# A patch-selection kernel that stores every tile first and finishes the kept rows afterwards by indirect transfers

## The chip, the cores and the metric

One core of a Trainium2 chip runs the whole program. The metric is device time in microseconds (us); lower is better. Before the change the median of three runs is 2007.05 us (2005.89 to 2010.34).

The core has TensorE (PE), VectorE (DVE), ScalarE (ACT), GpSimd (POOL) and SyncE (SP), which only issues transfers here. They run their own instruction lists and meet at semaphores. Indirect transfers, which gather or scatter rows by a list of row numbers, are issued by POOL.

## The reference

The input x is four images of 256 channels by 256 x 256 pixels, float32. A patch is 32 x 32 pixels, so an image has 8 x 8 = 64 places, each with one patch per channel. With `g = groupnorm(x)`:

```python
s = 0.5 * (|g[.., w+1] - g[.., w-1]| + |g[h+1, ..] - g[h-1, ..]|) + 0.5 * |g|   # zero padding of g
sp = mean of s over each 32 x 32 patch            # one score per channel and place
mask = (rank of sp among the 256 channels of the place) < 128
out = x + g * mask                                # mask is spread over the patch
```

The norm has 32 groups of 8 channels; mean and variance are over the group. A kept patch becomes `x * (1 + scale) + shift`, with scale and shift of its group, and the 128 patches that are not kept in a place are a plain copy of x.

## The kernel before

x lies in device memory as 64 tiles (16 per image) of 128 partitions by 8192 numbers, 4 MiB each. A tile is 16 channels by 8 bands of rows (the partitions) and 8 patches of 1024 pixels side by side (the free dimension). One row of 1024 numbers (4 KiB) is a patch in one partition; the indirect transfers move such rows.

**Analysis of a tile.** DVE takes the statistics (16 `bn_stats` of 512 columns, helper `statistics`, L911) one tile ahead; PE averages the mean over the group (`mean`, L680), and DVE writes its negative (`minus_mean`, L918). Then for each of the 8 patches: the sum of |x - mean| is made by ACT (L872, eight to a tile); the vertical differences by PE for 5 patches into PSUM (L707, L709), by DVE for one (L925) and by POOL for two (L355); the horizontal differences by POOL for all 8 (L349) into the buffers `pair` and `scratch`. The absolute values of the differences are summed by ACT (L866, L846, L855, L860) or by DVE (`place_sum`, L938). Columns and rows at the patches' edges have helpers of their own (L377 and L943, L689 to L696 and L948).

**Ranking.** After 16 tiles POOL and PE make the scale of each group; DVE multiplies the sums by it (`score`, L1080 and L1082), PE moves the scores so that the 64 places lie in partitions and the 256 channels in columns (L774), and DVE takes the 128 largest of each row in 16 rounds of `max` and `match_replace` (L1104, L1106). PE turns the mask back (L783), and DVE writes the coefficients (L1121 to L1126).

**Finishing, images 0 to 2.** While the next image is analysed, the tiles of the last one are read once more, in halves of 2 MiB, into three buffers `again`; ACT applies scale and shift to the whole half, kept or not (L803), and SP stores it. This is done for 27 halves of an image and, from the buffer `kept`, for its last tile. The 12 patches between are stored unchanged by a copy within device memory, and only their kept rows are gathered (L396), finished (L822) and scattered (L406). The constants `COPIES` place the 29 copies of halves in image 0, which has nothing else to finish.

**Finishing, image 3.** Ten tiles are copied within device memory early, and their kept rows are gathered, finished and scattered at the end (L521, L832, L530); the other six are finished as halves by DVE (L1178).

**Order.** It is written out by hand. ACT's list for a tile is a string such as `ORDER` (L102): `a` is a |x - mean| patch, `v` a vertical difference from PSUM, `o` a half to finish (4 instructions), `p` a group of gathered patches. POOL's list is `differences` (L411): it fills a first buffer and `scratch`, with at most one or two scatters behind the second of these, and the gathers behind the edge columns. Loops over tiles run through a ring of three buffers and `kept`.

Of the kernel before, what the change touches and what calls it, by code (L numbers as in the profile page):

```python
# [30 lines left out]

RING = 3
SLOTS = 3
LOOPED = (TILES - 1) // RING
LAST = TILES - 1
BN = 512
CHUNKS = PIX // BN

# [4 lines left out]
HALVES = 27  # L43
SPARSE_BETWEEN = [(h // 2, h % 2 * HALF_COLS + w) for h in range(HALVES, 2 * LAST) for w in range(HALF_COLS)]
SPARSE_STEP, SPARSE_GROUPS = 2, (1, 1, 1, 1, 1, 1, 1, 1, 2, 2)
assert sum(SPARSE_GROUPS) == len(SPARSE_BETWEEN) and sum(SPARSE_GROUPS[::2]) == sum(SPARSE_GROUPS[1::2])
PER_IMAGE = HALVES + 2
TURNS = HALVES // SLOTS

INSIDE = (PATCH - 2) * PATCH
PE_PATCHES = 5
DOWN_DVE, DOWN_POOL = 5, (6, 7)

PAIR_A, PAIR_B, SINGLE = range(3)
CONTENTS = {(PAIR_A, 0): (0, 1), (PAIR_A, 1): 7, (PAIR_B, 0): 6, (PAIR_B, 1): (3, 4), (SINGLE, 0): 2, (SINGLE, 1): 5}  # L60

ROUNDS = KEPT // 8
REC = 3 + COLS
INNER_ACROSS, INNER_DOWN, CENTRED, ROWS_AT_EDGE, COLUMNS_AT_EDGE = range(5)
KINDS = 5

ROWS = IMAGES * TILES * PARTS * COLS
NOT_A_ROW = 2 * ROWS
SPARSE_FIRST, SPARSE_END = 4, LAST - 1
SPARSE = SPARSE_END - SPARSE_FIRST
SPARSE_ORDER = [SPARSE_END - 2, SPARSE_END - 1, *range(SPARSE_FIRST, SPARSE_END - 2)]
SPARSE_BUFFERS = (0, 1, 2, 0, 3, 1, 2, 0, 3, 1)
SPARSE_PROGRAM = "S0 S1 G2 G3 G4 S2 G5 S3 G6 S4 G7 S5 G8 S6 G9 S7 S8 S9".split()
DENSE = [(LAST - 1, 0), (LAST - 1, 1), (LAST, 0), (LAST, 1), *((t, h) for t in range(SPARSE_FIRST) for h in range(2))]  # L80
DENSE_THERE = 4

MOVES_BEFORE_STORE = {4: 2, 5: 3, 6: 5, 7: 8, 8: 10, 9: 12, 10: 15, 11: 16}
MOVES_BEFORE_LOAD = {7: 4, 8: 6, 9: 9, 10: 11, 11: 13}
assert SPARSE_ORDER[:2] == [LAST - RING, LAST - RING + 1] and len(SPARSE_ORDER) == len(SPARSE_BUFFERS) == SPARSE


COPIED = [*(2 * TILES * (IMAGES - 1) + h for h in range(2 * SPARSE_FIRST, 2 * SPARSE_END)),
          *(2 * TILES * image + h for image in range(IMAGES - 1) for h in range(HALVES, 2 * LAST))]
COPIES = (0, 0, 1, 2, 2, 1, 2, 2, 1, 2, 2, 1, 1, 2, 2, 8)  # L90
assert sum(COPIES) == len(COPIED)


OUT, OUT_RANKING = (0, 2, 2, 2, 1, 2, 2, 1, 2, 2, 1, 2, 2, 2, 2, 0), 2
assert sum(OUT) + OUT_RANKING == HALVES and HALVES % SLOTS == 0

ORDER_FIRST = "A0 S0 d a0 B0 v0 a1 a2 v1 v2 a3 a4 a5 a6 v3 a7 v4".split()
ORDER = "o v0 a0 a1 a2 a3 a4 v1 a5 v2 d o a6 a7 v3 p v4".split()  # L102
ORDER_FIRST_LAST = "a0 v0 A0 a1 S0 v1 d a2 B0 a3 v2 a4 a5 v3 a6 a7 v4".split()
ORDER_LAST = "a0 v0 a1 v1 d a2 a3 v2 a4 a5 v3 a6 a7 v4".split()
ORDER_AFTER_RANKING = "a0 A0 v0 a1 d B0 v1 a2 A1 a3 v2 a4 a5 B1 a6 v3 a7 k k S0 S1 v4".split()


def halves_of(step):

    counts = (*OUT, OUT_RANKING)  # L110
    return range(sum(counts[:step]), sum(counts[:step + 1]))


def group_of(step):

    n = step - SPARSE_STEP
    return n if 0 <= n < len(SPARSE_GROUPS) else None


def patches_of(n):  # L120

    first = sum(SPARSE_GROUPS[:n])
    return [(p, *SPARSE_BETWEEN[p], n % 2 * HALF_COLS + p - first)
            for p in range(first, first + SPARSE_GROUPS[n])]


def patches_until(n, every=1):

# [3 lines left out]
def groupnorm_patch_topk(nc: bass.Bass, x: bass.AP, out: bass.AP):  # L132

    ctx = ExitStack()
    with ctx:
# [764 lines left out]
        def _(dve):  # L900
            def settle():
                dve.drain()  # L902
# [307 lines left out]
```

## Time and profile before

| | |
|---|---|
| median of 3 runs | 2007.05 us |
| span of the profiled execution | 2002.3 us |
| own time of it outside the span | about 4.8 us, the median less the span |
| PE, DVE, ACT, POOL busy | 1380.7, 1542.1, 1629.1, 1555.6 us |
| moved by DMA | 780.77 MB, mean 390 GB/s |
| row numbers of images 1 and 3 written (L1133, L1129) | at 867.9 and 1793.4 us |

The span runs from the first to the last instruction. A row of the page that ends in "x480 | 548.2, 1142" has 480 instructions, 548.2 us busy, 1142 ns each. In a timeline the first two columns are start and duration in us; durations of neighbours overlap by some 0.1 us, so what one instruction costs is the distance from its start to the next start. No engine is busy to the full, and the DMA engines are nearly so from 100 us to 1750 us.

### The profile page before, as it was taken

What the parts mean: (1) busy time and instruction counts of PE and PEld (TensorE: products, weight loads), DVE (VectorE), ACT (ScalarE), POOL (GpSimd) and SP (SyncE); (2) the same over time, 40 slices, a digit from 0 to 9 for tenths busy, and PEclk for the clock granted to TensorE, in tenths of its full rate; (3) what the DMA queues carried; (4) which work ended last, traced back from release to release, by engine and by line L of the source; (5) the groups of instructions that cost most, each with busy time, mean ns of one, the idle gap of its engine ahead of it and who ended that gap; (6) DMA issues with size and microseconds to landing.
All of it is one profiled execution on the core that took longest, in us unless ns stands there. A gap on an engine that the chain in (4) does not pass through costs nothing.

```text
span 2002.3 us, 16132 instructions
## 1 busy us (share of the span) xinstructions
PE 1380.7 (69%) x3528; PEld 675.7 (34%) x3528; DVE 1542.1 (77%) x2087; ACT 1629.1 (81%) x2437; POOL 1555.6 (78%) x1113
## 2 busy tenths in 40 slices
PE   5989989868768867857787687768688876820000
PEld 2444444434333433423333333334333333410000
DVE  7878898789898869879898977888888977872110
ACT  4999999898879888888898879889789887851643
POOL 7899899768787777758877868758878786746776
PEclk9999999988889878879888788889788887965555
DMA  5899899999999999998999999999999999969997
GB/s 252 330 399 369 333 360 392 354 403 424 429 432 430 422 362 433 390 415 365 428 430 429 432 399 389 433 389 386 430 430 432 426 400 390 381 267 397 397 368 270
DMA packets 72082, 780.77 MB, mean 390 GB/s; under 512 B 21883, under 2 KB 21883, under 8 KB 35648
## 3 DMA queue, kind: packets, MB, share of 16 engines
q1 hardware_dynamic: 40896, 723.54, 87.3%
q0 software_dynamic: 31104, 56.45, 7.5%
q14 instruction: 68, 0.56, 0.1%
q8 instruction: 14, 0.23, 0.0%
HBM read 568.33 MB, written 329.25 MB: 448 GB/s over the span
## 4 chain that ended last, share of the span: by engine, by line
issue 20%; DMA 19%; DVE 17%; POOL 16%; ACT 15%; PE 9%; DVEq 3%; POOLq 1%; ACTq 0%; SPq 0%
DVE stats L911 8%; DMA again<-in_x_dram 8%; POOL pair L349 5%; DMA ring<-in_x_dram 4%; ACT again L803 4%; DMA out_dram<-again 4%; DVE sums L938 4%; PE vertical L707 4%; ACT thrown L872 4%; PE vertical L709 4%; POOL pair L355 3%; DVEq L902 3%; ACT vertical L866 3%; DMA ring<-in_x_dram,pair 2%; POOL scratch L349 2%
## 5 line engine op out<-in xcount | busy, mean ns | idle before, releaser
L707 PE MATMUL vertical<-ring,plus 128*128 128x512 f32 (+1 forms) x1200 | 664.4, 638 | 241.9 <-ACT vertical L866 240.9
L349 POOL TENSOR_TENSOR pair<-ring 128x960 f32<-128x960 f32 x360 | 638.3, 1793 | 26.0 <-DVE scratch L1082 17.9
L709 PE MATMUL vertical<-ring,minus 128*128 128x512 f32 (+1 forms) x1200 | 634.0, 612 | 0.0
L911 DVE BATCH_NORM_STATS2 stats<-ring 128x6 f32<-128x512 f32 x960 | 582.4, 680 | 40.4 <-DMA ring<-in_x_dram 31.9
L872 ACT ACTIVATE thrown<-ring,record 128x1024 bf16<-128x1024 f32 x480 | 548.2, 1142 | 8.8
L938 DVE TENSOR_REDUCE sums<-pair 128x2 f32<-128x1920 f32 (+1 forms) x212 | 455.0, 2146 | 126.8 <-POOL pair L349 126.2
L803 ACT ACTIVATE again<-again,coef 128x1024 f32<-128x1024 f32 x324 | 374.4, 1227 | 107.2 <-DMA again<-in_x_dram 106.9
L707 PEld LDWEIGHTS vertical<-ring,plus 128*128 128x128 f32 x1200 | 240.9, 211 | 514.6 <-ACT vertical L866 292.4
L355 POOL TENSOR_TENSOR pair<-ring 128x960 f32<-128x960 f32 x120 | 270.5, 2254 | 141.8 <-DVE sums L938 116.3
L709 PEld LDWEIGHTS vertical<-ring,minus 128*128 128x128 f32 x1200 | 250.0, 208 | 295.5 <-issue 295.5
L349 POOL TENSOR_TENSOR scratch<-ring 128x960 f32<-128x960 f32 x120 | 215.3, 1794 | 152.8 <-ACT kept L822 103.3
L866 ACT ACTIVATE vertical<-vertical 128x960 f32<-128x960 f32 x320 | 303.6, 949 | 30.6 <-PE vertical L709 30.5
L832 ACT ACTIVATE ring<-ring,coef 128x1024 f32<-128x1024 f32 x64 | 73.1, 1226 | 114.5 <-DMA ring<-in_x_dram,pair 55.6
L925 DVE TENSOR_TENSOR vertical<-ring 128x960 f32<-128x960 f32 x60 | 109.0, 1817 | 39.4 <-ACT vertical L866 39.4
L938 DVE TENSOR_REDUCE sums<-scratch 128x1 f32<-128x960 f32 x106 | 119.1, 1123 | 4.2 <-POOL scratch L349 4.2
L1178 DVE TENSOR_SCALAR again<-again,coef 128x1024 f32<-128x1024 f32 x32 | 24.0, 822 | 121.2 <-DMA again<-in_x_dram 97.2
L680 PE MATMUL rank_bank<-record,averager 128*128 128x1 f32 x128 | 24.0, 257 | 119.6 <-DVE record L914 119.5
L530 POOL DMA_INDIRECT out_dram<-ring,pair x64 | 65.1, 1017 | 49.0 <-ACT ring L832 32.0
L872 ACT ACTIVATION_READ_ACCUMULATOR thrown<-ring,record 128x1 f32 x480 | 89.6, 187 | 0.0
L377 POOL TENSOR_TENSOR edges<-ring 128x448 f32<-128x448 f32 x60 | 81.5, 1359 | 0.8
L822 ACT ACTIVATE kept<-kept,coef 128x1024 f32<-128x1024 f32 x36 | 43.7, 1228 | 40.1 <-DMA kept<-in_x_dram,between_rows 40.1
L680 PEld LDWEIGHTS rank_bank<-record,averager 128*128 128x128 f32 x128 | 23.0, 207 | 152.3 <-DVE record L914 127.5
(118 smaller groups left out, 1443.2 us busy)
## 6 DMA issues: line engine op xcount, KB each, us to landing
ring<-in_x_dram SPq DMA_DIRECT2D x59, 4096.0 KB, 20.4
again<-in_x_dram SPq DMA_DIRECT2D x89, 2048.0 KB, 16.6
out_dram<-again SPq DMA_DIRECT2D x89, 2048.0 KB, 16.3
out_dram<-in_x_dram SPq DMA_DIRECT2D x29, 2048.0 KB, 28.6
kept<-in_x_dram SPq DMA_DIRECT2D x4, 4096.0 KB, 22.7
out_dram<-kept SPq DMA_DIRECT2D x8, 2048.0 KB, 13.8
ring<-in_x_dram SPq DMA_DIRECT2D x4, 1024.0 KB, 7.8
out_dram<-ring SPq DMA_DIRECT2D x2, 2048.0 KB, 9.7
```

The lines of the kernel that those rows point to most:

```text
L349: return nc.gpsimd.tensor_tensor(part.rearrange("p (r c) -> p r c", r=PATCH), xs[:, w, :, 2:], xs[:, w, :, 0:PATCH - 2], ALU.subtract)
L355: return nc.gpsimd.tensor_tensor(part, v[:, 2 * PATCH:], v[:, 0:INSIDE], ALU.subtract)
L377: nc.gpsimd.tensor_tensor(between.rearrange("p (w k r) -> p w r k", k=2, r=PATCH), xs[:, 1:, :, 0:2], xs[:, 0:COLS - 1, :, PATCH - 2:], AL ...
L707: nc.tensor.matmul(v[:, first:end], plus[:], xs[:, first + 2 * PATCH:end + 2 * PATCH], start=True, stop=False)
L709: done = nc.tensor.matmul(v[:, first:end], minus[:], xs[:, first:end], start=False, stop=True)
L803: done = nc.scalar.activation(v, v, ACT.Identity, scale=coef[:, bass.ds(t, 1), 0, w:w + 1].rearrange("p a w -> p (a w)"), bias=coef[:, bas ...
L832: nc.scalar.activation(v, v, ACT.Identity, scale=coef[:, t, 0, w:w + 1], bias=coef[:, t, 1, w:w + 1]).then_inc(sparse_finished, 1)
L866: done = nc.scalar.activation(v, v, ACT.Abs, accum_out=sums[r][:, INNER_DOWN, k:k + 1])
L872: nc.scalar.activation(thrown[:], patch(buffer, k), ACT.Abs, bias=record[r][:, 2:3], accum_out=sums[r][:, CENTRED, k:k + 1]).then_inc(cent ...
L911: nc.vector.bn_stats(stats[:, k, :], buffer[:, k * BN:(k + 1) * BN])
L925: nc.vector.tensor_tensor(down_dve, v[:, 2 * PATCH:], v[:, 0:INSIDE], ALU.subtract)\
L938: nc.vector.tensor_reduce(out, place[b], over, ALU.add, apply_absolute_value=True)\
```

## The change

The new kernel computes the same and is laid out anew. What changes, part by part:

1. **Storing.** Every tile is stored unchanged from the ring (`store_tile`) as soon as it is there, in all four images. Nothing is loaded a second time as halves, and nothing is copied within device memory (`COPIES` is all zero). The ring has four buffers. Excepted are "dense" tiles (`DENSE_FROM`): the last tile of images 0 to 2 and the last four of image 3 stay in the ring until their coefficients exist, are finished there and stored.
2. **Finishing.** For each of the 64 places of an image one indirect transfer gathers the 128 kept rows of the other tiles (partition = rank in the place), one ACT instruction finishes them, and one indirect transfer scatters them over the stored copy. Four places are a block; a block takes one of three buffers `slots`. A tile's step of image 1, 2 or 3 carries one block: POOL scatters block n-2 and gathers block n, ACT finishes block n-1. The 16 blocks of image 3 follow at the end.
3. **Lists.** DVE also writes which channels were picked (`max_index` in each of the 16 rounds, turned by PE in `turn_order`), the row numbers, and scale and shift of each picked row (`factors_of`, four times an image).
4. **Horizontal differences.** |a - b| is summed as 2 max(a, b) - a - b: DVE makes the sum of the maxima with one `scalar_tensor_tensor` with `accum_out` per patch (8 to a tile), and the sums of a and b come from the statistics and from the end columns (POOL adds 512 of them, DVE sums). POOL keeps three vertical differences a tile and ACT sums them. `place_sum` and its reductions on DVE, and DVE's own vertical difference, are gone. Only for the first tile of images 1 to 3, analysed beside the ranking, does POOL make all eight horizontal ones, with ACT summing.
5. **Loops** over tiles are unrolled.

```diff
-RING = 3
-SLOTS = 3
+RING = 4
+DENSE_FROM = (LAST, LAST, LAST, TILES - RING)
+COPIES = (0,) * TILES
+BLOCK = 4
+SETS = 3
-ORDER = "o v0 a0 a1 a2 a3 a4 v1 a5 v2 d o a6 a7 v3 p v4".split()
+ORDER = "p0 a0 v0 a1 p1 a2 o0 v1 a3 a4 o1 p2 v2 a5 o2 a6 v3 o3 a7 v4".split()
...
+            def gather_block(n):
+                image, first = n // BLOCKS, n % BLOCKS * BLOCK
+                pool.wait_ge(rows_ready, image + 1)
+                if n >= SETS:
+                    pool.wait_ge(scattered[n % SETS], 16 * BLOCK * blocks_before(n))
+                for j in range(BLOCK):
+                    row = rows[image % 2][:, first + j:first + j + 1]
+                    nc.gpsimd.indirect_dma_start(slot(n, j), None, x_rows,
+                                                 bass.IndirectOffsetOnAxis(ap=row, axis=0), bounds_check=ROWS - 1,
+                                                 oob_is_err=False).then_inc(gathered[n % SETS], 16)
...
+            for tile in range(ALL_TILES):
+                image, t = tile // TILES, tile % TILES
+                n = tile - TILES
+                if n >= 2:
+                    scatter_block(n - 2)
+                wait_loaded(pool, tile)
...
+                else:
+                    if n >= 0:
+                        gather_block(n)
+                    difference(tile, 0)
+                    end_columns(tile)
+                    difference(tile, 1)
+                    columns_at_edge(tile)
+                    difference(tile, 2)
...
+            scatter_block(STREAMED - 2)
+            scatter_block(STREAMED - 1)
+            for n in range(STREAMED, ALL_BLOCKS):
+                gather_block(n)
+                if n >= STREAMED + 1:
+                    scatter_block(n - 1)
+            scatter_block(ALL_BLOCKS - 1)
...
+            def store_tile(tile):
+                wait_loaded(sp, tile)
+                sp.dma_start(out[tile], ring[tile % RING][:]).then_inc(stored[tile % RING], 16)
...
+                for w in patches:
+                        nc.vector.scalar_tensor_tensor(out=larger[w % 2][:].rearrange("p (r c) -> p r c", r=PATCH),
+                                                       in0=xs[:, w, :, 2:], scalar=0.0, in1=xs[:, w, :, 0:PATCH - 2],
+                                                       op0=ALU.add, op1=ALU.max, accum_out=maxima[:, w:w + 1])
...
-                for _ in range(ROUNDS):
+                for k in range(ROUNDS):
                     nc.vector.max(largest[:], left)
                     settle()
+                    nc.vector.max_index(picked[:, 8 * k:8 * k + 8], largest[:], left)
                     nc.vector.match_replace(out=left, in_to_replace=largest[:], in_values=left, imm_value=-1.0)
```

DVE's step of a tile after the change, in its order: statistics of the next tile in four parts, the eight horizontal patches in four pairs between them, `keep_sums` of the tile before (which waits until ACT has done that tile), the end columns, edge rows, the negative mean of the next tile, edge columns, three small sums.

POOL before, in a step of images 1 to 3 (L349 and L355 fill buffers for the tile, L406 scatters, L396 gathers):

```order
L349 TENSOR_TENSOR pair<-ring 128x960 [waits place_free0]
L349 TENSOR_TENSOR pair<-ring 128x960
L402 ISA [waits copied]
L349 TENSOR_TENSOR scratch<-ring 128x960 [waits place_free2,between_finished]
L406 DMA out_dram<-kept,between_rows 65536x1024
L376 REGISTER_ALU
L377 TENSOR_TENSOR edges<-ring 128x7x32x2 [waits edges_free]
```

There two of the tile's differences stand ahead of the wait on `between_finished`, and one transfer follows it. POOL now, one step of images 1 to 3 and the start of the next (L372 scatters, L357 gathers, L320 makes a vertical difference, L333 the end columns, L343 to L347 the edge columns):

```order
L372 DMA out_dram<-slots,rows 65536x1024 [waits finished]
L372 DMA out_dram<-slots,rows 65536x1024 x3
L357 DMA slots<-in_x_dram,rows 128x1024 [waits scattered0,rows_ready,loaded2]
L357 DMA slots<-in_x_dram,rows 128x1024 x3
L320 TENSOR_TENSOR place<-ring 128x960 [waits place_free]
L333 TENSOR_TENSOR ends<-ring 128x512 [waits edges_free]
L320 TENSOR_TENSOR place<-ring 128x960 [waits place_free]
L343 TENSOR_TENSOR edges<-ring 128x7x32x2 [waits edges_free]
```

Eight transfers stand ahead of the tile's first difference, and the first of them waits for `finished`. ACT now, the end of one tile's list and the start of the next (L623 finishes a place, L653 sums one of POOL's differences, L659 one of PE's, L666 is |x - mean|):

```order
L666 ACTIVATE thrown,sums<-ring,record 128x1024 [waits centred]
L659 ACTIVATE vertical,sums<-vertical 128x960 [waits vertical_ready]
L623 ACTIVATE slots<-slots,offset,factor 128x1024
L666 ACTIVATE thrown,sums<-ring,record 128x1024 [waits centred]
L659 ACTIVATE vertical,sums<-vertical 128x960 [waits vertical_ready]
L653 ACTIVATE place,sums<-place 128x960 [waits place_ready,recorded]
L666 ACTIVATE thrown,sums<-ring,record 128x1024 [waits centred,minus_mean_ready]
```

The last place of a block (L623, which raises `finished`) stands two instructions ahead of the tile's end, and the next tile's list opens with a difference of POOL (L653), where before it opened with a half to finish.

## Rows read from the trace of the kernel before

**Rows 1.** The page, part 1 (engines' busy us) and part 2: GB/s in 40 slices.

```profile
PE 1380.7 (69%) x3528; PEld 675.7 (34%) x3528; DVE 1542.1 (77%) x2087; ACT 1629.1 (81%) x2437; POOL 1555.6 (78%) x1113
...
GB/s 252 330 399 369 333 360 392 354 403 424 429 432 430 422 362 433 390 415 365 428 430 429 432 399 389 433 389 386 430 430 432 426 400 390 381 267 397 397 368 270
```

**Rows 2.** The page, part 4: the chain that ended last, by engine.

```profile
issue 20%; DMA 19%; DVE 17%; POOL 16%; ACT 15%; PE 9%; DVEq 3%; POOLq 1%; ACTq 0%; SPq 0%
```

**Rows 3.** Stretches: us, busy PE, PEld, DVE, ACT, POOL, clock, DMA share, GB/s.

```profile
500.00:600.00 100.00, 71.17 (x172) 33.94 (x171) 86.83 (x108) 84.00 (x123) 81.47 (x56) 0.87 1.01 431
...
1850.00:1900.00 50.00, 0.00 (x0) 0.00 (x0) 8.88 (x12) 30.03 (x27) 35.79 (x37) 0.50 1.02 397
```

**Rows 4.** Groups of POOL by form: xcount | busy us, mean ns | idle before.

```profile
L355 POOL TENSOR_TENSOR pair<-ring 128x960 f32<-128x960 f32 x120 | 270.5, 2254 | 141.8 <-DVE sums L938 116.3 <-ACT pair L860 24.7
...
L396 POOL DMA_INDIRECT kept<-in_x_dram,between_rows x36 | 40.2, 1118 | 6.6 <-issue 6.6
L406 POOL DMA_INDIRECT out_dram<-kept,between_rows x36 | 39.8, 1104 | 6.5 <-issue 5.9
```

**Rows 5.** Timeline of POOL at the end: start, duration, instruction, idle before.

```profile
1884.33 0.97 POOL L530 DMA_INDIRECT out_dram<-ring,pair  x1 [0.30 <-issue]
1885.60 0.97 POOL L530 DMA_INDIRECT out_dram<-ring,pair  x1 [0.30 <-issue]
...
1994.47 0.97 POOL L530 DMA_INDIRECT out_dram<-ring,pair  x1 [0.31 <-issue]
```

**Rows 6.** Timeline of ACT in image 1.

```profile
601.88 1.15 ACT L872 ACTIVATE thrown<-ring,record 128x1024 bf16<-128x1024 f32 x1
...
603.15 1.15 ACT L872 ACTIVATE thrown<-ring,record 128x1024 bf16<-128x1024 f32 x1
...
604.30 0.95 ACT L866 ACTIVATE vertical<-vertical 128x960 f32<-128x960 f32 x1
...
605.27 1.13 ACT L872 ACTIVATE thrown<-ring,record 128x1024 bf16<-128x1024 f32 x1
...
613.85 4.62 ACT L803 ACTIVATE again<-again,coef 128x1024 f32<-128x1024 f32 x4
```

**Rows 7.** Timeline of ACT in image 0: a difference of POOL.

```profile
137.04 0.99 ACT L860 ACTIVATE pair<-pair 128x960 f32<-128x960 f32 x1
```

**Rows 8.** Timeline of DVE at the start.

```profile
23.15 4.84 DVE L911 BATCH_NORM_STATS2 stats<-ring 128x6 f32<-128x512 f32 x8 [4.53 <-DMA ring<-in_x_dram]
...
29.07 4.83 DVE L911 BATCH_NORM_STATS2 stats<-ring 128x6 f32<-128x512 f32 x8
33.98 0.59 DVE L914 BATCH_NORM_AGGREGATE record<-stats 128x2 f32<-128x96 f32 x1
34.48 0.63 DVE L948 TENSOR_REDUCE sums<-border_bank 128x8 f32<-128x512 f32 x1
```

**Rows 9.** DVE's two-input instruction, line L925: ns min/median/max.

```profile
L925 DVE TENSOR_TENSOR vertical<-ring x60: 1148/1198/4281, 27.9 to 1722.5; 128x960 f32<-128x960 f32 x60
```

**Rows 10.** The same line on the page, part 5: busy us, mean ns.

```profile
L925 DVE TENSOR_TENSOR vertical<-ring 128x960 f32<-128x960 f32 x60 | 109.0, 1817 | 39.4 <-ACT vertical L866 39.4
```

**Rows 11.** Timeline of DVE in the rankings of images 1 and 3.

```profile
834.36 1.16 DVE L1080 TENSOR_TENSOR scores<-records,scale 128x120 f32<-128x120 f32 x1
...
847.78 0.40 DVE L1106 MATCH_REPLACE8 scratch<-largest,scratch 64x256 f32<-64x256 f32 x1
...
864.31 2.35 DVE L1110 SCALAR_TENSOR_TENSOR scratch<-scratch,same_channel 64x1024 bf16<-64x1024 f32 x2
...
867.91 0.16 DVE L1133 SCALAR_TENSOR_TENSOR between_rows<-rank_bank,between_numbers 128x12 uint32<-128x12 f32 x1
...
1793.41 0.28 DVE L1129 SCALAR_TENSOR_TENSOR pair<-rank_bank,pair 128x128 uint32<-128x128 f32 x1
```

**Rows 12.** DMA issues: xcount, median us from issue to landing.

```profile
kept<-in_x_dram,between_rows POOLq DMA_INDIRECT x36, 18.3
```

More of the change, by code:

```diff
@@ L30 @@
 PATCHES = BANDS * COLS
-RING = 3
-SLOTS = 3
-LOOPED = (TILES - 1) // RING
+ALL_TILES = IMAGES * TILES
 LAST = TILES - 1
+RING = 4
 BN = 512
 CHUNKS = PIX // BN
[L43 to L48, printed above, removed]
@@ L88 @@
[L88 to L101, printed above, removed]
@@ L120, in patches_of @@
[L120 to L127, printed above, removed]
-    return sum(SPARSE_GROUPS[m] for m in range(n, -1, -every))
+INSIDE = (PATCH - 2) * PATCH
+DENSE_FROM = (LAST, LAST, LAST, TILES - RING)
+MOST_DENSE = TILES - min(DENSE_FROM)
+COPIES = (0,) * TILES
+COPIED_TILES = sum(COPIES) // 2
+assert sum(COPIES) % 2 == 0 and COPIED_TILES <= DENSE_FROM[-1]
@@ new lines, in scatter_block @@
+            def scatter_block(n):
+                image, first = n // BLOCKS, n % BLOCKS * BLOCK
+                if n % BLOCKS == 0:
+                    for b in range(RING):
+                        sent = [t for t in range(b, TILES * (image + 1), RING) if not (t // TILES == image and dense(t))]
+                        pool.wait_ge(stored[b], 16 * stores_until(sent[-1]))
+                    if image == IMAGES - 1:
+                        pool.wait_ge(copied, 16 * sum(COPIES))
+                pool.wait_ge(finished, n + 1)
+                for j in range(BLOCK):
+                    row = rows[image % 2][:, first + j:first + j + 1]
+                    nc.gpsimd.indirect_dma_start(out_rows, bass.IndirectOffsetOnAxis(ap=row, axis=0),
+                                                 slot(n, j), None, bounds_check=ROWS - 1,
+                                                 oob_is_err=False).then_inc(scattered[n % SETS], 16)
@@ new lines, in _, with copy_half @@
+            copies = [(TILES * (IMAGES - 1) + h // 2, h % 2) for h in range(sum(COPIES))]
+            def copy_half():
+                tile, h = copies.pop(0)
+                pixels = slice(h * HALF, (h + 1) * HALF)
+                sp.dma_start(out[tile, :, pixels], x[tile, :, pixels]).then_inc(copied, 16)
+            for quarter, signal in enumerate(first_loaded):
+                part = slice(quarter * PIX // 4, (quarter + 1) * PIX // 4)
+                sp.dma_start(ring[0][:, part], x[0, :, part]).then_inc(signal, 16)
@@ new lines, in _ @@
+            for tile in range(1, RING):
+                load_tile(tile)
+            for tile in range(ALL_TILES):
+                image, t = tile // TILES, tile % TILES
+                if ranked_beside(tile):
+                    for ahead in range(RING - 1):
+                        if not copied_tile(tile + ahead):
+                            store_tile(tile + ahead)
+                    store_finished(tile - 1)
+                elif not (dense(tile) or copied_tile(tile) or (image and t < RING - 1)):
+                    store_tile(tile)
+                if image == 0:
+                    for _ in range(COPIES[t]):
+                        copy_half()
+                if RING <= tile + RING - 1 < ALL_TILES:
+                    load_tile(tile + RING - 1)
@@ L776, in gather @@
                                              start=True, stop=True)
[L777 to L786 removed]
+                moved.then_inc(scores_moved, 1)
@@ L1061, in image_tiles @@
[L1061 to L1072 removed]
+                inner_across(tile, (6, 7))
```

1157 lines of the change are left out of this document (443 added, 714 removed).

## The prediction

> **What bounds the kernel now.** I read the page's slices first: from 100 us to 1750 us the transfers run at 333 to 433 GB/s, and the rate stays above 250 to the end [rows 1]. In a saturated stretch of image 1 the 16 DMA engines are busy throughout at 431 GB/s, with no engine of the core above 87% [rows 3]; at the end, with half of it indirect, they give 397. The chain of waits says the same by its mixture: no engine has more than a fifth [rows 2]. So the kernel is bound by transfers, and its engines wait a little everywhere. The bytes hardly change: the new kernel loads and stores 64 tiles of 4.19 MB (537 MB) and moves the kept half of 57 tiles twice (239 MB), 776 MB against 780.8. If the end only followed the bytes, nothing much would happen. What decides is whether the new lists can feed the transfers at that rate. I look at four stretches: image 0, a step of images 1 to 3, the ranking, the end.
>
> **Image 0.** Nothing is finished in it, and no copies fill it: 8.4 MB a step. DVE sets the step. Statistics: 4.83 us for eight [rows 8], 9.7 for 16. Aggregate 0.5 and means 0.15; three reductions of 512 columns (edge rows, edge columns, end columns) at 0.6, the distance of such a row to the next, 1.8; five small ones and five drains 1.15. Then eight maxima of 960 columns with a sum. No row has this form. The nearest is DVE's two-input subtraction of 960 columns: 1.148 us at best, 1.198 in the middle, 4.281 at worst [rows 9], 1.82 in the mean [rows 10]. The best is alone, about 1.08 from start to start; the rest is waiting for POOL, which was busy 78% [rows 1] and now is about 10 of 24 us (three differences of 2.25 [rows 4], end and edge columns 3.4), 41%: 0.62 x 41/78 = 0.33. I take 1.4 for one, 11.2 for eight. Bounds: 1.08, and 2.5 if the sum doubles the instruction and the waiting stays. A step is 24.5 us. ACT needs 18 us and is covered. From 23.15 us, when the second tile is there [rows 8], 16 steps end at 415.
>
> **The ranking.** From the scores to the row numbers DVE takes 33.6 us now, 834.36 to 867.91 [rows 11]. Out go two reductions of `place_sum` (2.1 each), a subtraction (1.1) and most of L1110, which then masks one tile and not 16 (2.1): 26.2. In come 16 `max_index`, whose nearest row is `match_replace`, 0.40 us [rows 11] and a load of its values, so 0.5 each and 8 us, and 3 us for turning the lists and adding the row numbers: 37 us. First coefficients: 415 + 37 = 452 us.
>
> **A step of images 1 to 3.** Here the order of the lists matters more than any duration. POOL's step begins with the scatter of block n-2, which waits for `finished`; ACT raises that with its last place, near the end of the tile before. Behind the waiting instruction stand four scatters, four gathers and only then the tile's first difference; and ACT's next tile opens with exactly that difference. So ACT cannot run while POOL issues, and POOL cannot start while ACT works: a ring of waits that is closed once per step.
> - POOL's part: an indirect transfer costs 1.27 us from start to start [rows 5]; in the middle of the flow 1.10 to 1.12 busy plus 0.18 idle [rows 4], 1.28 to 1.30. Eight are 10.4 us. The difference is a vertical one, 2.25 [rows 4]. With the two semaphores, 12.9.
> - ACT's part, first difference to last place: three differences at 0.98 [rows 7], seven |x - mean| at 1.13 to 1.27, four vertical ones at 0.97 [rows 6], four places at 4.53/4 = 1.13 with the last counted to its end, 1.23. Sum 19.6.
> - Step 32.5 us. ACT alone would need 21.9 (with the last two instructions), DVE 24.5, the transfers 12.6 MB / 431 GB/s = 29.2. All three are covered, and so is POOL's rest. The gathers are taken a step later, and even 18.3 us to landing [rows 12] is early enough.
>
> Bounds of the ring: an issue at 1.0 us (busy alone) gives 30.2; a waiting difference or a slower queue, 34.
>
> **An image's period.** After the coefficients POOL gathers a block, scatters the last one of the image before, gathers the second, makes a difference: 3 x 5.2 + 2.2 - 0.8 = 17 us until ACT starts the second tile. 14 steps follow to the start of the last: 455. That last tile ends 22 us on (DVE is held there by POOL's spread and the variance, and ends with ACT), then 37 of ranking. 17 + 455 + 22 + 37 = 531 us; before, (1793.4 - 867.9)/2 = 463 [rows 11]. The transfers carry 197 MB in it, 371 GB/s, so they have room. Coefficients of image 3: 452 + 3 x 531 - 3 (image 1 has no scatter at its start) = 2042 us.
>
> **The end.** 128 indirect transfers at 1.28 are 164 us of POOL; the first scatter waits 4 us for ACT; the last lands 8 us after its issue, as now (1994.5 to the span's end [rows 5]). Between a gather's last issue and its scatter lie eight issues, 10.4 us, for landing and 4.6 us of ACT; while the dense stores (16.8 MB, 40 us) fill the queues that fails for some blocks, 14 us. Sum 190; 176 without that, 215 if every block is late. Before, the end took 209 us (from 1793.4 [rows 11]), so this stretch gains some 20.
>
> **Sum.** 2042 + 190 = 2232 us of span against 2002.3; with the 4.8 us outside it 2237, against a median of 2007: 11% slower. What the change takes away (the second reading, the copies, much of POOL's arithmetic) was either hidden or comes back as indirect transfers, 512 of them, and those in the flow lie on the path.
>
> **Rivals.**
> - *The sum on DVE costs as much as the instruction.* Then one is 2.5 us, DVE's step 33.3. Image 0 grows by 16 x 8.8 = 141, and the steps of the flow by 42 x 0.8 = 34, the last tiles by 3 x 9: 2440. For it: no row shows a two-input instruction with its sum written out. Against it: L1110 does a two-input operation of 1024 columns at 1.2 us each (2.35 for two [rows 11]), and ACT's sums add 0.1 to 0.2 us, not a second pass. I hold the latter for nearer.
> - *Issues are short.* If an issue costs 1.0 us where other work stands around it, the ring is 30.2 us, near the 29.2 of the transfers; 42 steps less 2.3, 9 us less at the starts, 30 less at the end: 2100.
> - *Not slower: the ring of waits does not close.* If POOL stays a tile ahead (the difference is there when ACT asks), transfers bind. Place: between ACT's last place and its next difference; it decides from the point where eight issues and a difference take under 29.2 - 19.6 = 9.6 us. With maxima at 1.08 image 0 ends at 411; then three periods of 197 MB / 431 = 457, and 180 for the end: 1962 of span, 1967. For it: 431 GB/s is reached for 100 us on end [rows 3]. Against it: 12.9 us by the rows, and the order of the lists.
>
> The Trainium skill, "Vector Engine (DVE) Microarchitecture Reference", section "7. Points that are easy to get wrong", says that the scalar-tensor-tensor form with two SBUF sources that are not bf16 runs at half throughput because no read port is left for the accumulator. That is the first rival's case, and by it the time would be near 2440. L1110's rows have no accumulator, so the trace can't refute it; they only show the form itself at full rate.
>
> **Chances.** Forecast 0.63, first rival 0.14, short issues 0.15, not slower 0.08. The range of the forecast alone is 2170 to 2300: the issue's bounds (42 steps by +1.5 or -1), image 0 by the maximum's waiting (16 x 8 x 0.3 = 38), the end (-14, +25). The whole range reaches down to the short issues and up half-way to the first rival: 2085 to 2370; what is left out is the not-slower case and most of the first rival. A measurement of this kernel tells 0.2% (4 us) from no change. Of the 0.08, 0.07 is faster and 0.01 the same.
>
> **What would show it.** Right: in images 1 to 3 ACT idles about 10 us before the first difference of a tile, released by POOL; POOL idles before its scatter, released by ACT's place; steps of 32 to 33 us at about 390 GB/s; DMA share well below 1 in the ranking; maxima of 1.2 to 1.5 us; coefficients at about 452, 980, 1511 and 2042. Wrong: DVE waiting for loads in the flow (transfers bind), maxima above 2 us, or DVE busy throughout from 450 us on.

## The result, and the profile after

| | before | after |
|---|---|---|
| median of the runs | 2006.89 us | 2442.69 us (2438.68 to 2443.87) |
| profiled span | 2002.3 us | 2437.5 us |

The ratio is 1.216 (95% interval 1.2141 to 1.2178). The forecast was 2237 us, the range 2085 to 2370: the sign was right, the size was not. The coefficients of the four images are there at 491.0, 1077.6, 1669.4 and 2220.3 us (forecast: 452, 980, 1511, 2042). Of the span 2437.5 - 2232 = 205 us are missing in the forecast, and they fall into three stretches: 491.0 - 452 = 39 in image 0, (2220.3 - 491.0) - (2042 - 452) = 139 in the three periods, 217.2 - 190 = 27 at the end.

The page after: the engines' digits, the transfers (they answer to [rows 1]) and the chain [rows 2].

```profile
span 2437.5 us, 15496 instructions
PE 1430.6 (59%) x3503; PEld 693.4 (28%) x3503; DVE 1695.4 (70%) x3133; ACT 1445.7 (59%) x2377; POOL 1278.0 (52%) x1052
...
DVE  8999999897767676289776777349877776649000
...
DMA  9977875689899997739999999755999997325987
GB/s 413 405 286 301 319 310 241 276 353 395 358 378 366 360 364 291 306 135 422 386 364 364 365 360 371 291 215 224 424 360 365 363 379 277 129 77 221 368 301 267
DMA packets 93692, 777.02 MB, mean 319 GB/s; under 512 B 17560, under 2 KB 17560, under 8 KB 75936
...
ACT 31%; DVE 21%; issue 20%; POOL 20%; DMA 3%; PE 3%; POOLq 1%; DVEq 1%; SPq 0%; ACTq 0%
```

The bytes are as forecast (777 MB), the mean rate has fallen to 319 GB/s, and in the flow of images 1 to 3 it stands mostly at 360 to 379. In image 0, which moves only 8.4 MB a step, it falls to 241 to 319 once the ring is full; behind it the dips below 310 come once per image, in the slices about the ranking, and at the end. In the chain ACT now has 31%, and transfers 3%: they no longer bind.

The view of waits, all engines (who waited for whom, us in total, times, the longest):

```profile
ACT place L653 <- POOL place L320: 617.4, 57, 40.3
POOL out_dram L372 <- ACT slots L623: 594.5, 50, 22.1
...
DVE var L812 <- PE rank_bank L544: 143.9, 3, 60.3
...
ACT slots L623 <- DMA slots<-in_x_dram,rows: 125.8, 11, 35.0
...
POOL newton L383 <- issue: 84.9, 3, 41.8
```

The first two rows are the ring of waits. One turn of it, POOL's timeline in image 1 (start, duration, engine, line, instruction, the idle time before it and what ended it):

```profile
900.51 1.02 POOL L372 DMA_INDIRECT out_dram<-slots,rows  x1 [13.01 <-ACT slots L623]
901.83 0.98 POOL L372 DMA_INDIRECT out_dram<-slots,rows  x1 [0.30 <-issue]
...
907.06 1.82 POOL L357 DMA_INDIRECT slots<-in_x_dram,rows  x1 [0.31 <-issue]
...
911.48 2.22 POOL L320 TENSOR_TENSOR place<-ring 128x960 f32<-128x960 f32 x1
...
934.21 1.02 POOL L372 DMA_INDIRECT out_dram<-slots,rows  x1 [12.99 <-ACT slots L623]
```

and ACT's, the same turn:

```profile
880.10 1.00 ACT L653 ACTIVATE place<-place 128x960 f32<-128x960 f32 x1 [12.02 <-POOL place L320]
...
898.44 1.24 ACT L623 ACTIVATE slots<-slots,offset,factor 128x1024 f32<-128x1024 f32 x1
...
913.80 1.00 ACT L653 ACTIVATE place<-place 128x960 f32<-128x960 f32 x1 [12.01 <-POOL place L320]
```

ACT waits 12.0 us for the difference at 911.48, that stands behind eight transfers; POOL waits 13.0 us for ACT's last place at 898.44. Each is idle while the other works, and the step is 934.21 - 900.51 = 33.7 us (forecast 32.5). A window of image 1 and of the last tile's stretch (busy us of each engine, granted clock as a share of 2.4 GHz, share of the DMA engines, GB/s; the first answers to [rows 3]):

```profile
500.00:600.00 100.00, 74.56 (x178) 35.64 (x179) 86.41 (x156) 69.72 (x112) 54.40 (x42) 0.87 0.96 398
970.00:1020.00 50.00, 0.00 (x0) 0.00 (x0) 0.00 (x0) 4.34 (x8) 9.34 (x9) 0.50 0.99 411
```

The second is the surprise: for 50 us PE and DVE do nothing at all (the granted clock falls to its lower level, 1.2 GHz, in it), and the transfers are full. POOL's timeline there, and SyncE's queue:

```profile
978.62 0.99 POOL L357 DMA_INDIRECT slots<-in_x_dram,rows  x1 [0.30 <-issue]
979.64 2.22 POOL L320 TENSOR_TENSOR place<-ring 128x960 f32<-128x960 f32 x1
981.80 0.24 POOL L381 TENSOR_TENSOR spread<-records 128x16 f32<-128x16 f32 x1
1021.88 0.22 POOL L383 TENSOR_TENSOR newton<-spread 128x16 f32<-128x16 f32 x1 [39.84 <-issue]
```

```profile
969.33 0.33 SPq L457 DMA_DIRECT2D ring<-in_x_dram  x1
969.70 14.69 SPq L461 DMA_DIRECT2D out_dram<-ring  x3
```

Between L381 and L383 (two small steps of the spread, a part of the variance) stands only a drain, an instruction that holds POOL until its earlier work is done. In images 1, 2 and 3 the gap is 39.84, 41.77 and 3.31 us, the 84.9 us of the waits above. Image 3 has eight indirect transfers ahead of its drain too, but no tile is loaded or stored there. The periods show it too: 586.6, 591.8 and 550.9 us. PE's averaging waits for L385 behind it, DVE's variance (L812) for PE, and the ranking for that.

Image 0 on DVE, grouped by line, 0 to 430 us (busy us, mean ns; L719 is the maximum with its sum):

```profile
L719 DVE SCALAR_TENSOR_TENSOR larger<-ring 128x960 bf16<-128x960 f32 x120 | 160.2, 1372 | 5.0
L697 DVE BATCH_NORM_STATS2 stats<-ring 128x6 f32<-128x512 f32 x260 | 159.0, 680 | 10.3 <-DMA ring<-in_x_dram 9.2
L746 DVE SCALAR_TENSOR_TENSOR sums<-maxima,end_sums 128x8 f32<-128x8 f32 x15 | 29.5, 1968 | 1.1
L743 DVE SCALAR_TENSOR_TENSOR end_sums<-means,end_sums 128x8 f32<-128x8 f32 x15 | 20.7, 1381 | 1.7 <-issue 0.4
```

The maximum costs 1.37 us in the mean (forecast 1.4), so the first rival's mechanism is not there, though its number, 2440, is almost the time measured. But two sums of eight columns take 1.97 and 1.38 us. In DVE's timeline at 317.73 us they run beside POOL's end columns and a difference.

### The profile page after: what moved, and what is told of

It reads as the page before. It is cut to its first block, busy times and chain, and to the rows that moved or that the text cites. A ratio compares the mean times of both kernels' runs of the same rounds, so it can differ in the third digit from the quotient of the medians.

```text
span 2437.5 us, 15496 instructions
## 1 busy us (share of the span) xinstructions
PE 1430.6 (59%) x3503; PEld 693.4 (28%) x3503; DVE 1695.4 (70%) x3133; ACT 1445.7 (59%) x2377; POOL 1278.0 (52%) x1052
## 4 chain that ended last, share of the span: by engine, by line
ACT 31%; DVE 21%; issue 20%; POOL 20%; DMA 3%; PE 3%; POOLq 1%; DVEq 1%; SPq 0%; ACTq 0%
ACT thrown L666 14%; POOL slots L357 10%; ACT slots L623 8%; DVE larger L719 7%; ACT vertical L659 7%; DVE stats L697 6%; POOL place L320 5%; POOL out_dram L372 4%; ACT place L653 3%; DMA slots<-in_x_dram,rows 2%; DVE scratch L834 1%; DVE sums L746 1%; DVE largest L832 1%; PE vertical L537 1%; DVE scratch L835 1%
## 5 line engine op out<-in xcount | busy, mean ns | idle before, releaser
L537 PE MATMUL vertical<-ring,plus 128*128 128x512 f32 (+1 forms) x1280 | 734.0, 659 | 421.7 <-ACT vertical L659 421.3
L539 PE MATMUL vertical<-ring,minus 128*128 128x512 f32 (+1 forms) x1280 | 686.1, 620 | 0.0
L719 DVE SCALAR_TENSOR_TENSOR larger<-ring 128x960 bf16<-128x960 f32 x488 | 652.1, 1373 | 20.3
L697 DVE BATCH_NORM_STATS2 stats<-ring 128x6 f32<-128x512 f32 x1024 | 625.2, 679 | 12.8 <-DMA ring<-in_x_dram 9.2
L372 POOL DMA_INDIRECT out_dram<-slots,rows x256 | 259.1, 1012 | 662.9 <-ACT slots L623 594.5
L666 ACT ACTIVATE thrown<-ring,record 128x1024 bf16<-128x1024 f32 x512 | 583.1, 1139 | 3.1 <-DVE record L708 0.6
L653 ACT ACTIVATE place<-place 128x960 f32<-128x960 f32 x216 | 214.8, 994 | 617.4 <-POOL place L320 617.4
L320 POOL TENSOR_TENSOR place<-ring 128x960 f32<-128x960 f32 x192 | 434.2, 2263 | 43.7 <-ACT place L653 21.3
L659 ACT ACTIVATE vertical<-vertical 128x960 f32<-128x960 f32 x320 | 304.7, 952 | 188.4 <-PE vertical L539 187.8
L623 ACT ACTIVATE slots<-slots,offset,factor 128x1024 f32<-128x1024 f32 x256 | 309.8, 1230 | 156.6 <-DMA slots<-in_x_dram,rows 125.8
L357 POOL DMA_INDIRECT slots<-in_x_dram,rows x256 | 290.8, 1136 | 117.0 <-issue 76.6
L333 POOL TENSOR_TENSOR ends<-ring 128x512 f32<-128x512 f32 x61 | 94.9, 1555 | 215.2 <-DVE sums L730 215.2
L812 DVE TENSOR_SCALAR var<-rank_bank 128x16 f32<-128x16 f32 x4 | 0.7, 172 | 143.9 <-PE rank_bank L544 143.9
L666 ACT ACTIVATION_READ_ACCUMULATOR thrown<-ring,record 128x1 f32 x512 | 97.2, 190 | 0.0
L343 POOL TENSOR_TENSOR edges<-ring 128x448 f32<-128x448 f32 x64 | 88.8, 1388 | 0.0
L510 PEld LDWEIGHTS rank_bank<-record,averager 128*128 128x128 f32 x128 | 27.5, 239 | 201.0 <-DVE record L700 169.3
```

The source lines that it names most:

```text
L320: made = nc.gpsimd.tensor_tensor(out_place[:], v[:, 2 * PATCH:], v[:, 0:INSIDE], ALU.subtract)
L333: nc.gpsimd.tensor_tensor(ends[:], xs[:, :, :, 0:2], xs[:, :, :, PATCH - 2:], ALU.add)\
L357: nc.gpsimd.indirect_dma_start(slot(n, j), None, x_rows, bass.IndirectOffsetOnAxis(ap=row, axis=0), bounds_check=ROWS - 1, oob_is_err=Fals ...
L372: nc.gpsimd.indirect_dma_start(out_rows, bass.IndirectOffsetOnAxis(ap=row, axis=0), slot(n, j), None, bounds_check=ROWS - 1, oob_is_err=Fa ...
L537: nc.tensor.matmul(v[:, first:end], plus[:], xs[:, first + 2 * PATCH:end + 2 * PATCH], start=True, stop=False)
L539: done = nc.tensor.matmul(v[:, first:end], minus[:], xs[:, first:end], start=False, stop=True)
```

## The experiments

All ratios are against the kernel before on the same chip; the kernel after is at 2442.7. All are edits of the kernel after. The runs come from several chips, on which the kernel before lay at 2005.6 to 2012.7 us, so some 7 us between two of them mean nothing.

**Three causes, one at a time.** In POOL's list of an ordinary step the transfers move behind the first difference (e2), or behind two differences and the end columns (e1, shown):

```
-                    if n >= 0:
-                        gather_block(n)
                     difference(tile, 0)
                     end_columns(tile)
                     difference(tile, 1)
+                    if n >= 2 and middle:
+                        scatter_block(n - 2)
+                    if n >= 0:
+                        gather_block(n)
                     columns_at_edge(tile)
```

> Two differences and the end columns ahead of scatter and gather. Theory: the ring over the third difference is only 15.1 + 7.7 = 22.8 us, so it no longer binds; DVE (27 us as in image 0) and the transfers (12.6 MB at 431 GB/s, 29.2 us) do: steps of 29 to 30 us, 42 x -4.2 = -176, 2267 us. Rival (step set by DVE or transfers): 2443.

> The changed kernel (2442.7 us, step of images 1 to 3 33.7 us: 13.4 on POOL, 20.3 on ACT), with only the tile's first difference ahead of the scatter in the 42 ordinary steps. Theory (a ring of waits between ACT's last place and the next difference that stands behind eight transfers): the ring now closes over the second difference: 11.0 of transfers, 1.5 end columns, 2.2 difference, then 17.1 on ACT, 31.9 us; 42 x -1.8 = -76, 2367 us. Rival (the step is set by DVE or by transfers): no change, 2443.

Measured: e1 2396.2 us (1.194, 1.190 to 1.199), e2 2343.1 (1.168, 1.164 to 1.172). The smaller edit does what it should, and more: step 30.8 us (expected 31.9), ACT's wait 9.3, 100 us gone (expected 76). ACT's timeline of e2:

```profile
894.68 1.00 ACT L656 ACTIVATE place<-place 128x960 f32<-128x960 f32 x1 [9.29 <-POOL place L320]
...
925.50 1.00 ACT L656 ACTIVATE place<-place 128x960 f32<-128x960 f32 x1 [9.14 <-POOL place L320]
```

The larger edit gives only 46 us. In image 1 its steps are 31 to 32 us, then in images 2 and 3 they come in pairs of 67 us. Its waits, and ACT and SyncE there:

```profile
ACT slots L626 <- DMA slots<-in_x_dram,rows: 420.0, 28, 39.6
```

```profile
1254.42 1.24 ACT L626 ACTIVATE slots<-slots,offset,factor 128x1024 f32<-128x1024 f32 x1 [22.26 <-DMA slots<-in_x_dram,rows]
```

```profile
1269.88 0.33 SPq L460 DMA_DIRECT2D ring<-in_x_dram  x1
1270.25 0.63 SPq L464 DMA_DIRECT2D out_dram<-ring  x1
```

ACT waits for gathered rows, 22 us at a time. The gathers issued between 1273.67 and 1278.44, just behind a load and a store of a whole tile, are waited for again at 1322.08 (22.65 us), 43 us after their issue. A transfer has become what is late, though the rate is 302 GB/s in 1260 to 1290 us and 421 in the 30 us before. That was not in my theory.

In the last tile of an image, the spread and the scales ahead of that tile's transfers (e3); the three whole-tile stores no longer issued ahead of the ranking (e4); one more drain behind the gathers of the ninth tile of images 1 to 3 (e5):

```
-                if n >= 2:
+                if n >= 2 and t != LAST:
                     scatter_block(n - 2)
...
                 elif t == LAST:
-                    if n >= 0:
-                        gather_block(n)
                     difference(tile, 0)
                     partition_spread(image)
                     difference(tile, 1)
                     end_columns(tile)
                     scales(image)
+                    if n >= 2:
+                        scatter_block(n - 2)
+                    if n >= 0:
+                        gather_block(n)
```

```
-                    for ahead in range(RING - 1):
-                        if not copied_tile(tile + ahead):
-                            store_tile(tile + ahead)
                     store_finished(tile - 1)
+                    if not copied_tile(tile):
+                        store_tile(tile)
```

```
                         gather_block(n)
+                    if n >= 0 and t == 8:
+                        pool.drain()
                     difference(tile, 0)
```

> In the last tile of each image POOL makes the spread and the scales, with their drains, ahead of its eight transfers. Theory A (a drain of POOL waits until the transfers it issued have landed, and these queue behind a load and three whole stores, 21 MB): the waits of 41.8, 39.8 and 3.3 us go, 2443 - 85 = 2358 us. Rival B (POOL waits 40 us for something else there, DVE or the sequencer): no gain, 2443.

> The order of POOL stays; SP no longer stores three tiles ahead of the ranking, each tile is stored in its own step. Theory A: the drain then waits for a load and eight indirect transfers only, 8.4 MB or 20 us after their issue began, so 7 to 10 us in place of 40; 2 x -32, of which some is given back as a later backlog: 2380 to 2420 us. Rival B (not the transfers): the drain stays at 40 us.

> One drain of POOL is added behind the gather of block n in the middle step (t = 8) of images 1 to 3, where nothing else differs. Theory A (a drain waits until issued transfers have landed): it stops POOL until the gather lands, some 5 to 20 us, and the ring of waits hands this on: 2443 + 3 x 12 = 2480 us. Rival B (a drain settles POOL's arithmetic alone): under 1 us each, 2443.

Measured: e3 2338.2 us (1.165, 1.162 to 1.169), e4 2478.7 (1.235, 1.232 to 1.239), e5 2515.9 (1.254, 1.251 to 1.258). One row from POOL's timeline of e3 and one of e5, the instruction behind the drain:

```profile
972.90 0.21 POOL L383 TENSOR_TENSOR newton<-spread 128x16 f32<-128x16 f32 x1 [9.31 <-issue]
```

```profile
766.54 2.20 POOL L320 TENSOR_TENSOR place<-ring 128x960 f32<-128x960 f32 x1 [25.13 <-issue]
```

The added drain holds POOL for 25 us each time, and the time grows by 73: a drain does wait for the landing of the indirect transfers issued ahead of it. The counts of packets say so directly: in the kernel after the last indirect packet of image 1 moves between 1020 and 1021 us, and POOL goes on at 1021.88; in e5 between 763 and 764, and POOL goes on at 766.54. Moving them behind takes the drains of the kernel from 84.9 to 14.9 us and the time down by 104: 70 from the drains, and about 31 (my working, 3 x 10.4) since eight issues no longer stand ahead of each spread. The 9.31 us that are left in image 1 are not a landing: e3's last indirect packet moves before 961 us, the drain begins at 963.6. The same 9.31 stand in e7, e12 and e13; what they are is open. e4 takes the early stores away instead of the transfers, and the drains fall to 26.7 us: the stores are what the rows wait behind. But its time is 36 us more, a miss: the transfers idle in the ranking (67 and 83 GB/s in two slices), and the 37.7 MB, 92 us at 411 GB/s, come back in the flow, where ACT now waits 204.8 us for rows instead of 125.8. 58 less and 92 more is 34; that is a working, which no run takes apart.

**Image 0.** The small sums ahead of the edge columns, whose reduction sets POOL free:

```
-                columns_at_edge(tile)
                 finish_across(tile)
+                columns_at_edge(tile)
+                settle()
```

> DVE's small sums (two instructions of 8 columns with two inputs, 1.5 and 2.1 us in image 0) stand ahead of the reduction that sets POOL free for the end columns. Theory (they wait for a POOL instruction that reads the same memory; image 0 only, since in images 1 to 3 POOL is elsewhere then): they fall to 0.17 us, image 0 is 15 x 3.2 = 48 us shorter, the flow is unchanged: 2395 us. Rival (the collision only moves to the maxima): no change, 2443.

Measured: 2426.3 us (1.209, 1.206 to 1.213). DVE by line, 0 to 430 us:

```profile
L719 DVE SCALAR_TENSOR_TENSOR larger<-ring 128x960 bf16<-128x960 f32 x126 | 197.6, 1604 | 5.6 <-issue 0.4
...
L746 DVE SCALAR_TENSOR_TENSOR sums<-maxima,end_sums 128x8 f32<-128x8 f32 x15 | 2.5, 167 | 1.1
L743 DVE SCALAR_TENSOR_TENSOR end_sums<-means,end_sums 128x8 f32<-128x8 f32 x15 | 2.5, 167 | 1.4
```

The small sums fall from 50.2 us to 5.0, and the maxima rise from 1372 to 1604 ns, 29 us over 126. The small sums were long only for where they stood, beside POOL's list, and two thirds of that collision only move to the next two-input instruction of DVE; 16 us remain.

**All of it together, first try.** e7 is e1 and e3; e8 adds e6 and 24 copies of 2 MiB within DRAM in image 0 (`COPIES = (0, 0, *(2,) * 12, 0, 0)`), so that fewer tiles are stored later.

> Two differences and end columns ahead of the transfers in ordinary steps, and spread and scales ahead of them in the last tile. Theory: both gains add: 2443 - 176 - 85 = 2182 us.

> As the last, and the small sums ahead of the edge columns, and the 12 early tiles of image 3 copied within device memory during image 0 instead of stored from the ring. Theory: image 0 is 48 us shorter if the copies (50 MB) fit beside 134 MB in 440 us; in image 3 11 steps have 8.4 MB and are set by DVE at 27 instead of 29.5 us, -30: 2182 - 78 = 2104 us. Rival (copies slow image 0, since they load the memory twice): 2150.

Measured: e7 2321.2 us (1.157, 1.154 to 1.160), e8 2295.5 (1.144, 1.139 to 1.150). Both miss by 140 and 190. e7 has lost the drains (14.9 us) and most of POOL's wait for ACT (106.8 us instead of 594.5), and has in their place

```profile
ACT slots L628 <- DMA slots<-in_x_dram,rows: 416.7, 28, 34.7
```

**The late rows.** Two theories were left for e1: the transfers are full and all that was issued before the rows has to be done first, or a 4 KiB row takes turns with whatever the other queue has next, and the other queue's rows are of 32 KiB. So loads and stores of a tile are cut in eight, with the same bytes and rows of 4 KiB (e10 on the kernel after, e11 on e1):

```
-                sp.dma_start(ring[b][:], x[tile]).then_inc(loaded[b], 16)
+                for k in range(PIECES):
+                    p = slice(k * PIX // PIECES, (k + 1) * PIX // PIECES)
+                    sp.dma_start(ring[b][:, p], x[tile, :, p]).then_inc(loaded[b], 16)
```

> The changed kernel, with SP's loads and stores of a tile cut into eight transfers of one patch (rows of 4 KiB, as the indirect ones have, in place of 32 KiB). Theory C (the indirect transfers land late because a DMA engine takes turns between the queues by row, so that 4 KiB stand against 32 KiB): the drains at the rankings fall from 40 to some 15 us, 2443 - 50 = 2390 us; the ordinary step, where nothing waits for a landing, stays at 33.7. Rival D (they land late because all that was issued before them has to be done first): drains stay at 40 us, 2443 or a little more.

> Two differences and the end columns ahead of the transfers (2396 us, in images 2 and 3 two steps took 67 us, with 22 us of waiting for a gather that had been issued 43 us before), with loads and stores in pieces of 4 KiB rows. Theory C: the gathers land in time, all steps are 30 us as in image 1: 2396 - 28 x 3.7 - 50 = 2240 us. Rival D: 2396.

Measured: e10 2382.1 us (1.184, 1.182 to 1.187), e11 2272.4 (1.130, 1.127 to 1.132). POOL behind the same drain as above, in e10:

```profile
978.84 0.23 POOL L382 TENSOR_TENSOR spread<-records 128x16 f32<-128x16 f32 x1
992.95 0.21 POOL L384 TENSOR_TENSOR newton<-spread 128x16 f32<-128x16 f32 x1 [13.87 <-issue]
```

39.84 us have become 13.87, and all drains together 30.6 instead of 84.9, 54 of the 61 us that e10 gains. That alone would not part the two theories, since SyncE now takes 34 us to issue the three stores (from 971.25 us on), so fewer bytes stand ahead of the gathers. The packets do. Five microseconds inside the drain, 980 to 985 us, in the kernel after and in e10 (q1 is SyncE's queue, q0 the indirect transfers; packets, MB, share of the DMA engines):

```profile
q1 hardware_dynamic: 65, 1.61, 86.5%
q0 software_dynamic: 64, 0.25, 12.0%
```

```profile
q1 hardware_dynamic: 294, 1.07, 52.7%
q0 software_dynamic: 293, 1.01, 49.5%
```

In both the queues send one packet each in turn. With 32 KiB against 4 KiB the indirect transfers get 12% of the engines, with equal rows half. The third store of the kernel after is issued only at 984.06 us, behind the gathers, and yet they land after it: they don't merely wait for what was issued before.

And e1 at last loses its pairs of steps (31.2 us each now), and most waits for rows:

```profile
ACT slots L631 <- DMA slots<-in_x_dram,rows: 132.5, 11, 39.6
```

What sets 31.2 us is DVE. In e11's image 2, from 1140 to 1380 us, its small sums are as long as in image 0, since in e1's order POOL's differences stand beside them:

```profile
L754 DVE SCALAR_TENSOR_TENSOR sums<-maxima,end_sums 128x8 f32<-128x8 f32 x8 | 16.8, 2095 | 0.6
L751 DVE SCALAR_TENSOR_TENSOR end_sums<-means,end_sums 128x8 f32<-128x8 f32 x8 | 11.9, 1486 | 0.7
```

In the kernel after each takes 168 ns in the same window. So the expectation that in images 1 to 3 POOL is elsewhere holds only for the old order.

**The end.** The dense stores of the last four tiles are left out:

> Leaves out the last stores of image 3 (its four dense tiles, 16.8 MB), so the output lacks them. Theory (the end is 217 us and not 190 because gathers land late behind these stores: POOL waits 22 us at 2279 us): the end falls to 185 us, 2411 us. Rival (the chain of issue, landing and ACT sets each block anyway): under 8 us of gain.

Measured: 2409.5 us (1.198, 1.193 to 1.202), with 184 us from the last coefficients to the end instead of 217. Late rows behind dense stores are worth 33 us there. (Its output lacks those tiles.)

**What adds up, and the best version.** e12 is e2, e3 and e6; e13 is e1, e3, e6 and the pieces; e14 is e13 with the copies of e8.

> One difference ahead of the transfers in ordinary steps, spread and scales ahead of them in the last tiles, the small sums ahead of the edge columns. Theory: the three gains add, 2443 - 100 - 105 - 16 = 2222 us. The kernel before stays ahead at 2007, since image 0 and the rankings leave the transfers idle and a step still takes 31 us.

> Two differences and the end columns ahead of the transfers, spread and scales ahead of them in the last tiles, small sums ahead of the edge columns, rows of 4 KiB. Theory (the terms add): 2272 - 26 x 2 of drains - 16 = 2205 us. Rival (once one wait is gone the step is set by another, so they do not add): over 2240.

> The same, with the 12 early tiles of image 3 copied within device memory in image 0. Theory (transfers bind the flow at about 400 GB/s): image 3's steps fall from 31 to DVE's 27 to 28 us, 11 x 3.5 = -38, and image 0 grows by some 30 us as the copies made it do before (coefficients at 524 instead of 475 us): 2205. Rival (DVE binds the flow): image 0 grows and nothing comes back, 2240 us.

Measured: e12 2252.0 us (1.118, 1.114 to 1.121), e13 2135.7 (1.063, 1.060 to 1.065), e14 2172.1 (1.082, 1.080 to 1.084). e13 is the best version, 307 us better than the kernel after and still 6% slower than before. A window of image 2 in e1 with pieces (e11), in e13 and in e14:

```profile
1140.00:1380.00 240.00, 164.95 (x395) 81.71 (x396) 234.28 (x335) 168.31 (x279) 146.72 (x113) 0.82 1.01 399
```

```profile
1140.00:1380.00 240.00, 173.43 (x416) 85.94 (x417) 205.32 (x348) 179.66 (x298) 154.70 (x124) 0.84 1.02 411
```

```profile
1140.00:1380.00 240.00, 178.11 (x442) 88.34 (x440) 225.71 (x369) 185.33 (x309) 164.54 (x132) 0.87 1.03 418
```

In e13 the transfers are full at 411 GB/s (the kernel before reached 431 with its longer rows [rows 3]) and DVE is at 86% (98% in e11): two limits close together. The copies of e14 cost 36 us, as its rival had it (2240 against 2205): they put the first coefficients off from 475.6 to 533.3 us and give 34 of these 58 back by the last ones; in its image 3 DVE is busy 104.34 of 108 us and the DMA engines are not:

```profile
1609.00:1717.00 108.00, 85.48 (x212) 42.05 (x211) 104.34 (x174) 87.22 (x146) 77.68 (x61) 0.88 0.79 303
```

So lighter transfers alone gain little. e12 gave 30 us less than the sum of its parts, e13 69 more than expected. The traces show where: the expectation gave e6's edit 16 us, for image 0 alone, but in e1's order the small sums collide in every step (3.6 us of DVE in e11), and in e13 they take 168 and 167 ns in that window. Its steps are mostly 25.1 to 32 us, and its three periods together 110 us shorter than e11's, of which the expectation had 52. No run changes the place of the small sums alone in that order, so how the rest divides stays open.

## Why the prediction was right in kind and wrong in size

- **What bounds the kernel: right.** Bytes as forecast, and transfers no longer the limit.
- **The ring of waits: right, in place and nearly in size.** ACT 12.0 and POOL 13.0 us idle, each released by the other; 33.7 us against 32.5. ACT's leg is 20.4 us for 19.6; POOL's 13.3 for 12.9, since one of the four gathers takes 1.8 us. Over 42 steps it is 50 us, within the bound of 34 a step. e2 shows that the order alone is worth 100 us.
- **"That last tile ends 22 us on (DVE is held there by POOL's spread and the variance, and ends with ACT)": the step that failed.** I saw that DVE waits for POOL's spread, and priced the spread by its instructions. Behind L381 stands a drain, and ahead of it eight indirect transfers behind one load and three stores of a whole tile. It waited 85 us in all; with 50 for the steps that accounts for 135 of the 139 missing in the periods. In image 1 the last tile took 73 us from its first scatter to DVE's last small sum for the 22, 40 of them the drain. In image 3 it took 33 with a drain of 3.31, so some 8 to 11 us more were missing in it; that they don't show in the sum is luck, since the two steps behind a ranking were short (25.3 and 31.4 us in image 1). e3 and e5 show the mechanism, e4, e10 and the packets what it waits behind. The view of waits of before had a sign that this drain is not free, which I passed over, since the sum was small:

```profile
POOL newton L454 <- issue: 6.5, 4, 2.1
```

  Four drains waited up to 2.1 us with no indirect transfer just ahead of them. What the change had done is to put eight there. I had counted them as POOL's time for issuing, not as what a later instruction waits for.
- **Image 0: a mis-sized term.** The maximum was right (1.37 for 1.4), but the price of a collision with POOL was put on it alone. The small two-input sums, 0.17 us undisturbed, were counted among "five small ones" and took 3.35 together. So a step of 24.5 became 27.5 in most of image 0 (the one maximum a step that stands beside POOL's list, 3.17 us, is within the mean of 1.37): 39 us until the coefficients. e6 shows that the term belongs to the collision and not to an instruction.
- **The end: mis-sized.** "If every block is late" was my upper bound, 215, and it was 217, but not in that way: POOL was held up three times, by 22.11, 7.34 and 5.87 us, the first time when ACT waited 34.97 us for the rows of the third block. e9 gives 184 without the dense stores, where I had 176.
- **"even 18.3 us to landing [rows 12] is early enough": right here, wrong in general.** In the kernel after the gathers of the flow are never waited for (all 11 waits of ACT for rows lie behind 2190 us). Once the ring is loosened (e1), they take up to 43 us behind 32 KiB rows, and that wait eats what the order gives.
- **The first rival** ended on the right number by a mechanism that isn't there. By the Trainium skill, "Vector Engine (DVE) Microarchitecture Reference", section "7. Points that are easy to get wrong", the scalar-tensor-tensor form with two SBUF sources that are not bf16 has half the throughput. L719 has two float32 sources, a bf16 output and an accumulator, and takes 1.146 us at best and 1.157 in the median for 960 columns, and 0.082 us to read the sum, where L925 without a sum took 1.148 and 1.198 [rows 9]: the trace doesn't show the halving. The measurement decides.
- **Short issues** fell: the distance between issues is 1.30 us in the flow. **Not slower** fell too: even e13 with the ring opened is at 1.063.

## What to carry to other kernels

Before an indirect transfer is moved on POOL, look for each drain behind it: here it waited for the landing of every indirect transfer issued before, and the landing depended on what the other queue held and on how long its rows were. Where two engines with lists in fixed order wait for each other once per step, the step is the sum of both legs, and the cheapest cure is to put what the partner waits for ahead of what it doesn't. A wait that is taken away uncovers the next one: judge each edit together with the others (e1 gave 46 us alone, and 110 more over e10 once the rows were cut), not by adding up single gains.

## What the runs showed of the hardware

- A drain on POOL behind eight indirect transfers waited 40 us with a load and three stores of 4 MiB in the other queue, 14 when these came in 4 KiB rows, 25 in the middle of the flow, and 3.3 with nothing in the other queue.
- Two queues with work sent packet for packet: 65 against 64 in 5 us with 32 KiB against 4 KiB, 294 against 293 with 4 KiB both.
- An indirect transfer of 128 rows of 4 KiB holds POOL for 1.30 us from start to start; in the step shown one of the four gathers took 2.1.
- A two-input instruction of DVE on eight columns takes 0.17 us alone and 1.4 to 2.1 us when POOL's two-input instructions run back to back; moved away, two thirds of the wait fall on the maxima behind it (mean 1372 to 1604 ns).
- In PE's idle stretch of 50 us the granted clock was 0.50, against 0.87 in the flow. The clock was not the cause of the loss: PE had nothing to do, it waited for POOL's L385.
